# First batch of a grouped-weights layer: x loaded in two halves, the first weight chunk two k at a time

## What is computed

```python
def cond(x, weight, adapter_ids):          # x (8, 256, 1024), weight (8, 1024, 1024)
    return einsum('bsi,boi->bso', x, weight[adapter_ids])

def ffn(h, gate_w, w_gate_up, w_down, shared_w_gate_up, shared_w_down):
    g, u = split(h @ shared_w_gate_up.T);  shared_out = silu(g) * u @ shared_w_down.T
    probs = softmax(h @ gate_w.T);         combine = the two best, divided by their sum
    g, u = split(einsum('th,eih->eti', h, w_gate_up))
    out_e = einsum('eti,ehi->eth', silu(g) * u, w_down)
    return einsum('eth,te->th', out_e, combine) + shared_out

out = x + ffn(cond(x, weight, adapter_ids), ...)
```

## Time and profile before

| | us |
|---|---|
| median of 3 runs (1063.51 to 1063.78) | 1063.52 |
| the profiled execution, as timed | 1062.65 |
| its span in the trace | 1060.7 |
| PE busy in the span | 1053.1 (99%) |
| DVE busy | 634.6 (60%) |
| ACT busy | 457.7 (43%) |

### The profile page before, as it was taken

The page is one execution under the profiler, slowest core; times in us unless marked ns, Lnnn a source line. Parts: engine busy times, 40 slices in busy tenths (PEclk is TensorE's granted clock), DMA queues, the critical chain, the costliest instruction groups (busy, mean ns, idle before and its releaser), DMA issues.

```text
span 1060.7 us, 15852 instructions
## 1 busy us (share of the span) xinstructions
PE 1053.1 (99%) x4817; PEld 870.3 (82%) x4818; DVE 634.6 (60%) x652; ACT 457.7 (43%) x529; POOL 275.6 (26%) x325
## 2 busy tenths in 40 slices
PE   8999999999999999999999999999999999999998
PEld 7888888888888888888888888888888888888887
DVE  5766765636756667876766867353553446544454
ACT  6565644532223556665655755332223222322310
POOL 1000000000036655555555650130003200032040
PEclk9999999999999999999999999999999999999999
DMA  8999877422256779986987865763656336464355
GB/s 330 348 365 350 298 282 266 180 80 80 92 211 208 281 269 343 341 331 241 377 346 261 291 242 205 257 219 119 154 224 238 138 119 188 189 238 146 111 192 204
DMA packets 55782, 248.03 MB, mean 234 GB/s; under 512 B 8194, under 2 KB 21634, under 8 KB 45954
## 3 DMA queue, kind: packets, MB, share of 16 engines
q1 hardware_dynamic: 29826, 161.50, 42.5%
q0 software_dynamic: 19008, 62.41, 16.9%
q10 hardware_dynamic: 6912, 23.66, 5.7%
HBM read 200.87 MB, written 43.52 MB: 230 GB/s over the span
## 4 chain that ended last, share of the span: by engine, by line
PE 99%; DMA 1%; SPq 0%; DVE 0%; issue 0%; ACT 0%
PE bank L588 32%; PE bank L590 32%; PE bank L589 32%; PE bank L613 1%; PE bank L826 1%; DMA raw<-cond_w 1%; PE bank L601 0%; PE bank L759 0%; PE bank L622 0%; DMA ids<-ids 0%; SPq L350 0%; PE bank L746 0%; PE bank L794 0%; DVE w_split_sb L1225 0%; DVE rows L1490 0%
## 5 line engine op out<-in xcount | busy, mean ns | idle before, releaser
L1225 DVE TENSOR_TENSOR w_split_sb<-raw,w_split_sb 128x2048 fp32r<-128x2048 f32 (+3 forms) x154 | 257.5, 1703 | 59.7 <-ACT w_split_sb L912 59.2
L912 ACT ACTIVATE w_split_sb<-raw 128x2048 fp32r<-128x2048 f32 (+3 forms) x154 | 216.0, 1439 | 64.2 <-PE bank L590 53.5
L527 POOL DMA_INDIRECT h_in<-h_dram,idx_h x156 | 176.2, 1130 | 124.0 <-DVE tile_f L1539 80.3
L588 PE MATMUL bank<-hT_hi,w_split_sb 128*128 128x512 f32 x512 | 199.8, 390 | 0.0
L589 PE MATMUL bank<-hT_lo,w_split_sb 128*128 128x512 f32 x512 | 199.3, 389 | 0.0
L590 PE MATMUL bank<-hT_hi,w_split_sb 128*128 128x512 f32 x512 | 199.3, 389 | 0.0
L588 PE MATMUL bank<-w_split_sb,tile_hT 128*128 (+1 forms) x312 | 124.8, 400 | 0.0
L590 PE MATMUL bank<-w_split_sb,tile_hT 128*128 (+1 forms) x312 | 122.0, 391 | 0.0
L589 PE MATMUL bank<-w_split_sb,tile_hT 128*128 (+1 forms) x312 | 121.8, 390 | 0.0
L590 PEld LDWEIGHTS bank<-hT_hi,w_split_sb 128*128 128x128 f32 x512 | 96.2, 188 | 20.0
L589 PEld LDWEIGHTS bank<-hT_lo,w_split_sb 128*128 128x128 f32 x512 | 96.2, 188 | 19.8
(11 more groups left out here) (153 smaller groups left out, 1417.6 us busy)
## 6 DMA issues: line engine op xcount, KB each, us to landing
raw<-sh_gu_w SPq DMA_DIRECT2D x16, 2048.0 KB, 9.1
raw<-exp_gu_w SPq DMA_DIRECT2D x16, 2048.0 KB
raw<-cond_w SPq DMA_DIRECT2D x13, 2048.0 KB, 10.1
y_dram<-y_out ACTq DMA_DIRECT2D x39, 512.0 KB, 4.0
raw<-sh_down_w SPq DMA_DIRECT2D x8, 2048.0 KB, 7.7
raw<-exp_down_w SPq DMA_DIRECT2D x16, 1024.0 KB, 8.4
h_dram<-h_blk POOLq DMA_DIRECT2D x16, 512.0 KB, 9.1
x_raw_sb<-xT SPq DMA_DIRECT2D x7, 1024.0 KB, 9.5
```

The lines of the kernel that those rows point to most:

```text
L527: nc.gpsimd.indirect_dma_start(out=h_in[par][:, i, :], out_offset=None, in_=h_blocks, in_offset=bass.IndirectOffsetOnAxis(ap=idx_h[par][:, ...
L588: nc.tensor.matmul(dst, lhs[0], rhs[0], start=first, stop=False)
L912: return nc.scalar.activation(dst, src, ACT.Copy)
L1225: return nc.vector.tensor_tensor(dst, src, hi.bitcast(F32), ALU.subtract)
```

## The change

The first chunk's eight DMAs of one k-block become four of two k-blocks (512 KB each, list `W_FIRST`), with one semaphore each. The four DMAs of x become two of 512 KB: the first is issued at once, the second behind ACT's copy of weight block 0, where the fourth stood. ACT's copies, DVE's subtractions and PE's matmuls keep their sizes, their order and their counts; ACT waits for an x half ahead of pieces 0 and 2, and for a weight DMA ahead of blocks 0, 2, 4 and 6.

```diff
-    WPIECE_K = KT // W_PIECES
+    W_FIRST = [(0, 2), (2, 4), (4, 6), (6, 8)]
...
             def first_loads():
                 a = sp.value_load(small["ids"][0:1, 0:1], min_val=0, max_val=ADAPTERS - 1)
-                for i in range(PIECES):
-                    for k in (2 * i, 2 * i + 1):
-                        c0, c1 = k * WPIECE_K * HALF, (k + 1) * WPIECE_K * HALF
-                        sp.dma_start(raw[0][:, c0:c1], cond_w[bass.ds(a, 1), 0, :, c0:c1].rearrange("o p n -> (o p) n")).then_inc(first_w[k], 16)
+                for i, (k0, k1) in enumerate(W_FIRST):
+                    c0, c1 = k0 * HALF, k1 * HALF
+                    sp.dma_start(raw[0][:, c0:c1], cond_w[bass.ds(a, 1), 0, :, c0:c1].rearrange("o p n -> (o p) n")).then_inc(first_w[i], 16)
...
             def first_x_load(i):
-                act.dma_start(x_raw_sb[:, i * PIECE_K * SEQ:(i + 1) * PIECE_K * SEQ],
-                              xT[0, :, i * PIECE_K * SEQ:(i + 1) * PIECE_K * SEQ]).then_inc(first_x[i], 16)
-
-            for i in range(2):
-                first_x_load(i)
+                x0, x1 = i * KX // 2, (i + 1) * KX // 2
+                act.dma_start(x_raw_sb[:, x0:x1], xT[0, :, x0:x1]).then_inc(first_x[i], 16)
+
+            first_x_load(0)
...
             for i in range(PIECES):
-                act.wait_ge(first_x[i], 16)
+                if i % 2 == 0:
+                    act.wait_ge(first_x[i // 2], 16)
                 k0, k1 = i * PIECE_K, (i + 1) * PIECE_K
                 copy(x_split_sb[0][:, 0, k0:k1, :].rearrange("p k t -> p (k t)"), x_raw_sb[:, k0 * SEQ:k1 * SEQ]).then_inc(first_hi, 1)
-                if i == 0:
-                    first_x_load(2)
                 for k in (2 * i, 2 * i + 1):
-                    act.wait_ge(first_w[k], 16)
+                    for landed, (k0, _) in zip(first_w, W_FIRST):
+                        if k0 == k:
+                            act.wait_ge(landed, 16)
                     copy(w_split_sb[:, 0, 0, k * HALF:(k + 1) * HALF], raw[0][:, k * HALF:(k + 1) * HALF]).then_inc(first_hi, 1)
                     if k == 0:
-                        first_x_load(3)
+                        first_x_load(1)
```

More of the change, by code:

```diff
@@ L173, in adaln_ffn_kernel @@
         gate_lo_done = sem("gate_lo_done")
-        first_x = [sem(f"first_x{i}") for i in range(PIECES)]
-        first_w = [sem(f"first_w{i}") for i in range(W_PIECES)]
+        first_x = [sem(f"first_x{i}") for i in range(2)]
+        first_w = [sem(f"first_w{i}") for i in range(len(W_FIRST))]
         second_w = [sem(f"second_w{i}") for i in range(4)]
```

## The result

The changed kernel takes 1067.83 us (median of 6 runs, 1066.17 to 1069.26), the kernel before 1063.51 (6 runs, 1062.96 to 1063.78): 1.0042 of it, 95% interval 1.0031 to 1.0053. The prediction was 1065.4 with a range of 1062.8 to 1068.6, and 52% for slower by over 0.2%. The time lies in the range, which had been drawn wide enough for the rivals, but the change costs 4.3 us where the forecast had 1.9. The scatter has grown as well, from 0.8 to 3.1 us, which will matter.

The account below looks back on a forecast made before the run. PE's start plus a fixed row of matmuls was taken as the bound. k = 4 moving from 15.10 to 17.0 us, with no new wait behind, added 1.9 us to 1063.52: 1065.4 us, range 1062.8 to 1068.6.

Parts of the forecast that it names:

- What bounds the kernel: Whole kernel: PE's start plus a fixed row of matmuls; only the first 15 us count, 2.2 us of waits to win.
- Part 1: First weight DMA, now 512 KB: lands at 7.0 us (6.4 to 7.5), PE begins at 8.5 us, 0.6 later.
- Part 2: Blocks 2 and 3 land at about 9.2 us; the 1.38 us wait at k = 2 goes, by itself 0.9 us won.
- Part 3: Second half of x, needed at k = 4: lands at 14.9 us, PE at 17.0 instead of 15.10, cost 1.9 us.
- transfers of the two queues are served in the order of issue: Start of kernel: a load on ACT's queue waits for all that SP has issued before it.
- The sum: Bytes landed with x's half: 1 MB of x, 2 MB, 512 KB of the second chunk; 16.2 us as upper bound.
- the gain by longer packets: Early DMA stretch, 4.4 to 9.5 us: less idle time between packets, 1.3 us off x's landing at 16.2 us.
- Part 4: Behind k = 4: no new wait, the shift stays as it is to the end, +1.9 us.
- Behind one more: Rival, 25%: SP's sixth weight DMA gets in front of x's half; 1.3 us more, cost 3.2 us, 1066.7 us.
- Shared from the issue on: Rival, 14%: queues take turns at once, x's half lands at 11.7 us, k = 4 at 14.2; 0.9 us won, 1062.6.
- The clock falls: Rival, 13%: PE's idle time at k = 4 lowers its clock, costing 0.7 to 1.8 us more; 1066.7 us.

Follow-up runs that it names:

- the changed kernel again: The changed kernel unaltered, measured once more on another chip (its profile is the second trace): 1067.43 us, 1.0041.
- the weights alone: Against the kernel before: first weight chunk in four pieces of two k-blocks, x still in four pieces at the old places; 1063.29 us, 1.0003.
- the held chunk: Changed kernel, but SP issues the second weight chunk's four loads only once blocks 2 and 3 have landed; 1063.29 us, 1.0002.
- the half at the third place: Changed kernel with x's second half issued behind the copy of x for k = 0 and 1, where the third piece stood; 1062.53 us, 0.9997.
- the one row: Kernel before, with x's third and fourth piece issued by SP among its weight DMAs: 1061.89, then 1062.10 us; with the second piece too, 1062.26 us.
- the filler kernel: Changed kernel with 45 small matmuls on the tile of ones ahead of PE's wait at k = 4; 1066.04 us, 1.0025.
- x alone: Against the kernel before: x in two halves, the second behind the copy of weight block 0, weights still in eight pieces; 1064.77 us, 1.0017.
- the whole chunk: Changed kernel with the second weight chunk in one DMA of 2 MB instead of four of 512 KB; 1069.3 us, a single run.

## Why the prediction was right, and where its terms were off

The mechanism held in its main part: one wait moves, to k = 4 and to the late half of x, and the kernel gets longer by it. Two things in it failed. The loads are not served in the order of issue, and the cost was 4.3 us instead of 1.9, 3.0 for x and 1.3 for a clock that the forecast had left to a rival.

*What bounds the kernel* held: nothing behind the first 25 us explains the difference; the changed kernel is 6.35 us late at `gate_pair` and 6.1 at the end. Waits of 0.2 to 0.9 us further on, in the experts' stage, up to 1.5 us together, appear in some profiled executions (of the changed kernel again, the weights alone, the held chunk, the half at the third place, the one row) and are missing in others; they are part of the scatter.

*Part 1, the first weight DMA.* Forecast: landed at 7.0 us, 7.5 at most. It was 8.1, and 7.7 in the second trace: outside the bound. The step that failed is taking one execution's 6.4 and 7.5 us for the arrival of blocks 0 and 1. In four other traces with the old piece of 256 KB, block 0 came at 6.3, 7.6, 7.9 and 8.1 us. The trace of before was an early one, and one row is no bound for an arrival in this stretch.

*Part 2, no wait at k = 2.* Right, in every kernel in which the third piece of x didn't stand in front.

*Part 3, the second half of x.* The place was right: one wait, at k = 4, back over ACT's copy of x to a DMA of 8.4 us (forecast: near 8). The rule behind it, "transfers of the two queues are served in the order of issue", is the step that failed. The trace of before contradicts it: its fourth piece of x, issued at 6.4 us, had its first packet at 9.9, and from 10 to 11 us the two queues moved almost alike:

```profile
q1 hardware_dynamic: 122, 0.22, 56.1%
q10 hardware_dynamic: 95, 0.19, 48.0%
```

What the runs show instead is a wait of 3.4 to 3.7 us for the first packet, then turns. That the landing came out near was luck. The sum put one DMA of the second chunk ahead of x. By 8.1 us SP had issued all four, and strictly in that order x would have landed behind the last of them, at 20.0 us; since the queues take turns it landed behind the first alone. Two errors cancelled.

The size was short: landed at 16.5 us instead of 14.9, PE at 18.62 (17.71 in the second trace) instead of 17.0. The issue at 8.1 us instead of 7.0 is no term of that sum; the term at fault is the gain by longer packets, put at 1.3 us. The rate went from 239 to 300 GB/s in 4.4 to 9.5 us, worth 5.1 x (1 - 239/300) = 1.0, but in 9.5 to 12.5 us it was 351 instead of 395 GB/s, which takes back 0.3. With 16.2 - 0.7 = 15.5 us the second trace agrees (15.6). The first is another 1 us later, and its second chunk's first DMA too: in both, x lands 0.4 us behind that (15.2 and 16.1 us). Why this execution was later isn't shown. In place of 1.9 us the late x costs 2.6 to 3.5, 3.0 by the median of the filler kernel.

*Part 4, no new wait behind it*: right.

*The rivals.* "Behind one more" didn't come in that form: by 8.1 us SP had issued three more DMAs, not one, but x landed ahead of all three. Its reason was right: SP's issues no longer stalled as long (1180 ns for the sixth before, 339 now). "Shared from the issue on" is half right: the turns it names are there, but they begin 3.7 us after the issue, not at once, and so the small gain that it promised didn't come. "The clock falls", given 13%, happened in eight of eleven runs. Its price was forecast as 0.7 to 1.8 us: 1.5 in two traces (x alone, the whole chunk), 2.8 in that of the changed kernel. The step that failed is its likelihood and not its existence: the idle time was worked out as 2.8 us, which became 3.3 in one trace and was 2.8 in the other, the one without a fall.

## What to carry to other kernels

A load issued when something else has landed waits until the other issuing engine's queue has moved on (3.4 to 3.7 us here), and then shares with all that is still under way. So ask what is in front of it and beside it, in bytes, look at the packets of each queue and not at landings alone, and hold back what is needed later. Fusing the loads at this kernel's start won nothing: for the weights it was worth nothing, and the fused load of x, issued behind a wait, cost 3 us and a fall of the clock; issued behind the first copy of x it cost nothing that could be measured. Price a new gap on TensorE twice, as the gap and as a stretch at half clock behind it; where it can't be closed, small matmuls in it can keep the clock up, as in all seven runs here.

## What the runs showed of the hardware

The gaps on PE after which the granted clock stood at 0.50: 2.96, 3.33, 4.24 and 5.48 us; without a fall: 2.80 us and less. That the clock was left at the upper level after 2.80 us in one run and gone after 2.96 in another fits the runs of one and the same kernel, of which some fall and some don't.

How long the clock stayed down under dense matmuls doesn't go by the gap: some 6 us after the two short ones (10.9 to 16.9 us, 18.6 to 24.4), 3 us after the two long ones (19.35 to 22.3, 20.9 to 23.8). The price was 2.8 us in the changed kernel and 1.5 with x alone and with the whole chunk (there 5.81 us late at k = 4 and 7.26 at `gate_pair`). In the changed kernel the clock fell at 17.6 us (0.81 in 17 to 18), 2.3 us after PE's last matmul. With x alone (columns as above):

```profile
21.00:22.00 1.00, 1.00 (x3) 0.76 (x3) 1.00 (x3) 1.00 (x2) 0.00 (x0) 0.50 0.56 66
22.00:23.00 1.00, 1.00 (x5) 0.83 (x4) 1.00 (x2) 1.00 (x2) 0.00 (x0) 0.83 0.82 328
```

From 4.4 to 9.5 us the DMAs don't reach their rate, with any size of piece: 231 to 263 GB/s in five traces with weights at 2 KB to a partition, 294 to 311 in seven at 4 KB (345 with both halves of x in front), against 395 at 2 KB a little later. Doubling the piece won a fifth to a quarter there. Why the early stretch is slow, the runs don't say.
